# A fused AdaLN, Mamba scan and tree-FFN kernel: softplus of delta straight from PSUM, half of dt in another bank, and three jobs moved in a 32-step schedule

## What is computed

```python
sa, ca, ga, sb, cb, gb = silu(c) @ wmod        # per batch; gates kept at least 0.25 in size
h = layernorm(x) * (1 + ca) + sa
xp, z = split(h @ W_in)                         # 256 channels each
u = silu(causal_depthwise_conv(xp, 4 taps) + conv_b)
dt_r, B, C = split(u @ W_xp, [8, 24])           # rank 8, 16 states for B and for C
delta = softplus(dt_r @ W_dt + dt_bias)
h_t = exp(delta_t * A) * h_(t-1) + delta_t * B_t * u_t      # 256 channels x 16 states
y_t = sum over n of h_t[n] * C_t[n] + u_t * D
x = x + ga * ((y * silu(z)) @ W_out)
h = layernorm(x) * (1 + cb) + sb
gate = sigmoid(h @ (routers Wq))                # 255 nodes of a tree of depth 8
leaf_prob = product of gate or 1 - gate along the path to each of 256 leaves
x = x + gb * (leaf_prob @ leaf_values @ Wout.T + b)
```

## Time and profile before

| | |
|---|---|
| three runs | 538.68 us median (534.51 to 538.88) |
| the profiled execution's own time | 538.69 us |
| its span | 536.9 us |
| mean granted TensorE clock | 0.898 |
| busy: PE, DVE, ACT, POOL | 406.6 (76%), 454.3 (85%), 374.1 (70%), 445.3 us (83%) |
| POOL `hc` L561 | 126 of 2367 ns |
| DVE scan L1286 | 192 of 1270 ns and 64 of 1210 ns |
| DVE `dbu` L1299 | 80 of 1206 ns |
| POOL `dbu` L548 | 48 of 2363 ns |
| ACT exp L649 | 256 of 684 ns |

### The profile page before, as it was taken

How to read it: one execution, slowest core, us unless ns; L and a number is a source line. 1 busy time by engine, 2 the same in 40 slices (tenths; PEclk the granted TensorE clock), 3 DMA queues, 4 the chain that set the end, 5 groups by cost and what they waited for, 6 DMA issues and landing times. The chain is left out here.

```text
span 536.9 us, 6647 instructions
## 1 busy us (share of the span) xinstructions
PE 406.6 (76%) x2104; PEld 278.4 (52%) x2135; DVE 454.3 (85%) x542; ACT 374.1 (70%) x680; POOL 445.3 (83%) x246
## 2 busy tenths in 40 slices
PE   8978834896679757984899747984899758574887
PEld 4436524483548435663567435662557435464554
DVE  6788794998999968998799968997899968998871
ACT  3367774478966888588756898598856886448454
POOL 3468889999899978997799979997889978998800
PEclk8989885899799969998799979999899969785899
DMA  6491062200721073303512063303512063300001
GB/s 169 132 357 75 6 235 89 106 2 21 249 106 62 6 236 117 99 0 125 208 34 89 5 236 117 100 1 131 202 43 81 6 234 118 98 0 2 8 13 39
DMA packets 24867, 53.16 MB, mean 99 GB/s; under 512 B 4601, under 2 KB 13952, under 8 KB 20736
## 3 DMA queue, kind: packets, MB, share of 16 engines
q1 hardware_dynamic: 24832, 52.74, 29.0%
HBM read 50.11 MB, written 2.62 MB: 98 GB/s over the span
## 5 line engine op out<-in xcount | busy, mean ns | idle before, releaser
L561 POOL TENSOR_TENSOR hc<-h,c_rows 128x1024 f32<-128x1024 f32 x126 | 296.6, 2367 | 41.4 <-DVE h L1286 38.0
L1286 DVE TENSOR_TENSOR_SCAN h<-dA,state,dbu 128x512 f32<-128x512 f32 x192 | 234.6, 1270 | 20.1 <-ACT dA L649 19.8
L649 ACT ACTIVATE dA<-delta,a_neg 128x512 f32<-128x512 f32 x256 | 173.1, 684 | 44.5 <-DVE h L1286 43.6
L1065 PE MATMUL yb<-ident,hc 128*128 128x128 f32 x1024 | 155.8, 291 | 22.0 <-POOL hc L561 20.1
L1065 PEld LDWEIGHTS yb<-ident,hc 128*128 128x128 f32 x1024 | 133.3, 152 | 64.7 <-issue 32.4
L548 POOL TENSOR_TENSOR dbu<-du,b_rows 128x1024 f32<-128x1024 f32 x48 | 113.4, 2363 | 4.0 <-DMA b_rows<-bc_dram 4.0
L1299 DVE TENSOR_TENSOR dbu<-du,bb 128x1024 f32<-128x1024 f32 x80 | 96.5, 1206 | 20.5 <-PE bb L1090 10.9
L1286 DVE TENSOR_TENSOR_SCAN h<-dA,dbu 128x512 f32<-128x512 f32 x64 | 74.6, 1210 | 17.8 <-ACT dA L649 17.7
L973 PE MATMUL mf<-f_hT,w_conv 128*128 128x512 f32 x112 | 56.1, 628 | 2.0 <-ACT zu L708 1.4
L996 PE MATMUL mf<-zu,w_xdt 128*128 128x512 f32 x56 | 31.2, 640 | 17.1 <-ACT delta L742 11.5
L824 PE MATMUL mt<-ident,t_xhat 128*128 128x128 f32 x28 | 7.6, 427 | 37.8 <-ACT t_xhat L590 37.8
(11 more groups left out here) (198 smaller groups left out, 544.5 us busy)
## 6 DMA issues: line engine op xcount, KB each, us to landing
c_rows<-bc_dram SPq DMA_DIRECT2D x32, 1024.0 KB, 6.8
b_rows<-bc_dram SPq DMA_DIRECT2D x48, 256.0 KB, 7.3
xs<-in_L_attn_x_dram SPq DMA_DIRECT2D x8, 256.0 KB, 3.8
out_dram<-xs SPq DMA_DIRECT2D x7, 256.0 KB, 5.6
ygT<-in_L_attn_conv_w_dram SPq DMA_DIRECT2D x1, 512.0 KB, 5.1
bc_dram<-xd SPq DMA_DIRECT2D x8, 64.0 KB, 1.6
probT<-in_L_wmod_dram SPq DMA_DIRECT2D x1, 384.0 KB, 4.0
w_in<-in_L_attn_W_in_dram SPq DMA_DIRECT2D x1, 256.0 KB, 4.2
```

The lines of the kernel that those rows point to most:

```text
L561: nc.gpsimd.tensor_tensor(hc[:, pair % RC, :, :], h[:, pair % RH, :, :], c_rows[:, q, n % NQ, :].unsqueeze(1).broadcast_to([P, HALVES, T]) ...
L649: nc.scalar.activation(dA[ke % RD][:, :], delta[:, ge % 2, half, :], ACT.Exp, scale=a_neg[:, half, n:n + 1]).then_inc(s_dA, 1)
L1065: last = nc.tensor.matmul(bank[:, tile], hc[:, pair % RC, half, tile], ident[:, :], start=False, stop=n == N - 1, is_transpose=True, skip_ ...
L1286: v.tensor_tensor_scan(h[:, pair % RH, half, :], dA[k % RD][:, :], dbu[:, pair % RW, half, :], start, ALU.mult, ALU.add).then_inc(s_scan, 1)
```

## The change

Five edits:

1. ACT no longer copies `dt` to SBUF. Softplus with the bias reads the product from PSUM, one instruction per half, at step 17.
2. `dt` half 1 is a job of the t bank (same PE steps 13 and 14), since the f bank now stays occupied by half 0 until step 17. `xd` therefore goes to PE steps 18 and 19 and is read at step 20.
3. The path sums `lp` move to PE steps 19 and 21, `ff` to 23 and 24, the final add to DVE step 24; they now come before the rows' turn: `t_xhat` moves from 19 to 24 (its factor from 15 to 19, POOL's offset from 16 to 20), its `tr` to 27, `node` to 29 and 30.
4. The first norm's statistics of a group are taken one group earlier at step 19 (group 2's before the first scan), and its factor, offset and `f_xhat` at steps 2, 3 and 6.
5. The turns and products of the tail's weights in group 0 move some steps forward.

```diff
-    N_STATS, N_RSTD, N_OFF, N_XHAT = 19, 21, 22, 25
-    F_SILU, F_DT, F_SP, F_DU = 10, (13, 15), 17, (25, 26)
+    N_STATS, N_RSTD, N_OFF, N_XHAT = 19, 2, 3, 6
+    F_SILU, F_SP, F_DU = 10, 17, (25, 26)
-    T_GATE, T_ADD, T_STATS, T_RSTD, T_OFF, T_XHAT = (4, 5), 12, 12, 15, 16, 19
-    U_FIN = 28
+    T_GATE, T_ADD, T_STATS, T_RSTD, T_OFF, T_XHAT = (4, 5), 12, 12, 19, 20, 24
+    U_FIN = 24
     "f": ...
-              ("dt", 0): (1, (11, 12)), ("dt", 1): (1, (13, 14)), ("xd", 0): (1, (15, 16)), ("tr", 0): (2, (28,))},
-        "t": {("yt", 0): (-1, (6,)), ("yt", 1): (-1, (8,)), ("out", 0): (-1, (10,)), ("tr", 0): (-1, (20,)),
-              ("lp", 0): (-2, (22,)), ("lp", 1): (-2, (24,)), ("ff", 0): (-2, (25, 26)), ("node", 0): (-1, (28,)),
-              ("node", 1): (-1, (30,))},
+              ("dt", 0): (1, (11, 12)), ("xd", 0): (1, (18, 19)), ("tr", 0): (2, (28,))},
+        "t": {("yt", 0): (-1, (6,)), ("yt", 1): (-1, (8,)), ("out", 0): (-1, (10,)), ("dt", 1): (1, (13, 14)),
+              ("lp", 0): (-2, (19,)), ("lp", 1): (-2, (21,)), ("ff", 0): (-2, (23, 24)), ("tr", 0): (-1, (27,)),
+              ("node", 0): (-1, (29,)), ("node", 1): (-1, (30,))},
-    W_TURN, W_COPY, W_MUL, W_TAKE, W_SCALE = (4, 9), (7, 11), 13, 16, 20
+    W_TURN, W_COPY, W_MUL, W_TAKE, W_SCALE = (3, 7), (5, 9), 10, 12, 20
...
+        def wait_delta(eng, g, half):
+            if g == 0:
+                eng.wait_ge((s_d0, s_delta)[half], 1)
+            else:
+                wait_read(eng, "ft"[half], "dt", half, g)
...
-                    if front and s in F_DT:
-                        half = F_DT.index(s)
-                        wait_job(act, "f", "dt", half, f)
-                        nc.scalar.activation(delta[:, f % 2, half, :], job("f", "dt", half, f)[1][:, :], ACT.Identity,
-                                             bias=dtb[:, half:half + 1]).then_inc(s_read["f", "act"], 1)
                     if (front or leaf) and s == F_SP:
                         if front:
-
-                            wait_read(act, "f", "dt", 1, f)
-                            both = delta[:, f % 2, :, :]
-                            nc.scalar.activation(both, both, ACT.Softplus).then_inc(s_delta, 1)
+                            for half in range(HALVES):
+                                side = "ft"[half]
+                                wait_job(act, side, "dt", half, f)
+                                nc.scalar.activation(delta[:, f % 2, half, :], job(side, "dt", half, f)[1][:, :],
+                                                     ACT.Softplus, bias=dtb[:, half:half + 1]).then_inc(s_read[side, "act"], 1)
...
-                    if norm and s == N_STATS:
+                    if 2 <= g + 3 < GROUPS and s == N_STATS:
                         dve.wait_ge(s_x, 16 * (GROUPS - 2))
-                        stats(m2, f_bn, f_mv, s_fvar)
+                        if g >= 0:
+                            dve.wait_ge(s_fnm, g + 1)
+                        stats(g + 3, f_bn, f_mv, s_fvar)
```

More of the change, by code:

```diff
@@ L79, in bass_adaln_mamba_tree_ffn_kernel @@
     AHEAD_EXP, AHEAD_FILL, AHEAD_DBU, LAG_SUM = 2, 3, 2, 5
-    N_STATS, N_RSTD, N_OFF, N_XHAT = 19, 21, 22, 25
-    F_SILU, F_DT, F_SP, F_DU = 10, (13, 15), 17, (25, 26)
+    N_STATS, N_RSTD, N_OFF, N_XHAT = 19, 2, 3, 6
+    F_SILU, F_SP, F_DU = 10, 17, (25, 26)
     F_HI, F_R1, F_MID, F_R2, F_LO = 21, 22, 23, 24, 25
-    T_GATE, T_ADD, T_STATS, T_RSTD, T_OFF, T_XHAT = (4, 5), 12, 12, 15, 16, 19
-    U_FIN = 28
+    T_GATE, T_ADD, T_STATS, T_RSTD, T_OFF, T_XHAT = (4, 5), 12, 12, 19, 20, 24
+    U_FIN = 24
     JOBS = {
         "f": {("xp", 0): (1, (0, 1)), ("xp", 1): (1, (3, 4)), ("z", 0): (1, (7,)), ("z", 1): (1, (8,)),
[3 rows of a table removed]
-              ("node", 1): (-1, (30,))},
[3 rows of a table added]
+              ("node", 0): (-1, (29,)), ("node", 1): (-1, (30,))},
     }
     BY_DVE = {"out", "ff"}
+    FIRST_BY_HAND = {("f", "xp"): 1, ("f", "dt"): 1, ("t", "dt"): 1, ("f", "xd"): 1, ("f", "tr"): 2}
     Z_OF_0 = (29, 30)
     TR_OF_1 = STEPS - 1
-    W_TURN, W_COPY, W_MUL, W_TAKE, W_SCALE = (4, 9), (7, 11), 13, 16, 20
+    W_TURN, W_COPY, W_MUL, W_TAKE, W_SCALE = (3, 7), (5, 9), 10, 12, 20
     WARM_START = 9
@@ L112, in bass_adaln_mamba_tree_ffn_kernel @@
             for (name, part), (off, steps) in sorted(JOBS[side].items(), key=lambda job: job[1][1]):
-                first = {"xp": 1, "dt": 1, "xd": 1, "tr": 2}.get(name, 0) if side == "f" else 0
-                if first <= g + off < GROUPS:
+                if FIRST_BY_HAND.get((side, name), 0) <= g + off < GROUPS:
                     job_at[side, name, part, g + off] = len(read_at[side])
@@ L564, in _ @@
                         half = F_DU.index(s)
-                        pool.wait_ge(s_delta, f + 1)
+                        wait_delta(pool, f, half)
                         pool.wait_ge(s_silu, f + 1)
@@ L642, in _ @@
                         if se < HALVES:
-                            act.wait_ge(s_delta, ge + 1)
+                            wait_delta(act, ge, se)
                         if ke >= RD:
@@ L995, in product @@
                         pe.wait_ge(s_silu, g + 1)
+                        if (side, g) == ("t", 1):
+                            pe.wait_ge(s_wtake, 1)
                     last = nc.tensor.matmul(bank[:, :], w_xdt[:, piece, part * P:(part + 1) * P],
```

## The result

The changed kernel takes 516.05 us (median of four runs, 514.96 to 541.32) against 538.36 us for the kernel before, run beside it: a ratio of 0.959, 95% interval 0.954 to 0.965, so 4.1 per cent faster. The forecast was 520.1 us. (The run of 541.32 was disturbed and is left out of the ratio.) The profiled execution took 514.96 us, 23.7 less than the profiled one of before, where the sum said 18.6.

What follows compares the result with a forecast made beforehand. DVE's 53.5 us a cycle plus its stalls was taken as the bound, POOL's 54.0 close under. Gains 14.8 - 0.8 + 2.25 + 1.9 + 0.5 = 18.6 us, from 538.7 to 520.1 us; range 510 to 538.

Steps and rivals of the forecast that it cites:

- Bound: Whole cycle of 60.6 us: DVE's 53.5 us plus its stalls bound it, POOL's 54.0 a floor close under.
- Softplus from PSUM: ACT's block at step 17: 0.6 us pipelined per half, block ends 1.3 us earlier, step 20 stall falls by 1.4.
- Path sums: PE steps 19 to 24: the 2.06 us stall for bb goes; DVE's add waits 1.0 us for ff, bounds nothing and 5.0.
- the hand walk: Group 3 reckoned step by step: ff ready at 260.4, DVE there at 260.0, a wait of 0.5 us at the add.
- First norm: Factor and f_xhat moved to the first half of ACT's cycle: cost nothing; if cover fails, up to 1 us a cycle.
- Sum: Stalls per cycle from 6.6 to 2.9 us (step 20 1.4, ff 1.0, silu 0.5): gain 3.7, cycle 56.9.
- The start's term: Group 2's statistics now ahead of the first dbu: between 0 and 1.6 us lost, 0.8 taken.
- The clock rival: TensorE at 1.2 GHz over lp and ff: DVE waits 5.0 us at the add, no gain, 538 us; chance 0.10.
- Half of it: ACT reads xd and path sums later, the add's wait becomes 3 us, a cycle gains 1.7: 530 us; chance 0.20.
- slower: DVE stands twice around the add, for exp (1.5) and ff (5.0): about 549 us (543 to 553); chance 0.10.
- `xd` late for POOL: xd's later read makes POOL wait for its rows; 9 us of cover against it, counted within the slower case.
- POOL's floor: All stalls but the block's go, POOL hardly waits: 54.5 us a cycle, 508 us; chance 0.05.

Runs made afterwards that it cites:

- the filler products: Ten zero-matrix products on PE at step 18, before xd: changed kernel 521.87 us; dbu before step 20's scan 521.77; that with the add at 26 509.99.
- two edits later: Changed kernel with DVE's dbu ahead of the scan at step 20 and the final add at step 26: 508.19 us, ratio 0.943 to the kernel before.
- the kernel with the `dbu` first: Changed kernel with DVE's dbu ahead of the scan at step 20, add still at step 24: 519.41 us, ratio 0.964 to the kernel before.

## Why the prediction was right, point by point

**Bound.** DVE plus its waits, with POOL close under it: held. DVE's work hardly changed, its waits in four cycles fell by 14.3 us, and POOL's gaps followed.

**Softplus from PSUM.** Taken at 0.6 pipelined, measured 0.58. In group 3 the step-20 stall was to fall to 1.4: it is 1.40. Over the groups it is not so even: 1.40, 1.40, 1.58, 2.58 and 2.58 us in groups 2 to 6. In the last two DVE has no statistics of a coming group left to take at step 19, and stands where in the others it works: I had overlooked that the statistics fill part of the stall, and that one more group is without them after the change. `xd`'s later read cost POOL nothing: no wait for the spread rows is in its list. But the step "its stall falls, so the cycle gains" fails for this edit taken alone (0.1 us a cycle against 1.1 in company): it needs the path sums out of the turn's way.

**Path sums.** The waits at `bb` went, as the hand walk had it, but for one of 0.4 us. The wait at the add was put at 1.0 us, bounds 0 and 5.0, and is 0.23 to 0.72, 0.45 a cycle in the stretch. The walk itself had given 0.5; the doubling I put on it for caution was not needed.

**First norm.** "Cost nothing" holds for the change as a whole, by the run without it. Its silu stall stayed under 1.2 us (0.32 to 1.12), and no wait was added.

**Sum.** Waits 3.0 us a cycle against 2.9. That they agree so well is luck, for the terms do not: step 20 is 1.74 (forecast 1.4), the silu block 0.75 (0.5), `bb` 0.1 (nothing), the add 0.45 (1.0). Three came out too small and one too large by nearly as much. The four cycles gained 16.7 against 14.8: the waits gave 14.3 of it and DVE's work 2.2, where the forecast had only waits. About 1.25 of the work is the set of statistics, for which the stall of group 5 is longer. Outside them the start, forecast at 1.45 with group 1, was measured at 3.4, of which half is no merit of the change (below), and the last group's 0.5 at 1.7, inside its bounds.

Group 0 went as foretold: its long ACT wait (6.28 us in the kernel before) is gone, and DVE stands for POOL in its place, at one scan for POOL's late `dbu` and then for `du` (1.95 in the earlier trace rows):

```profile
85.26 1.22 DVE L1291 TENSOR_TENSOR_SCAN h<-dA,dbu 128x512 f32<-128x512 f32 x1 [8.02 <-POOL dbu L555]
...
92.29 1.22 DVE L1304 TENSOR_TENSOR dbu<-du,bb 128x1024 f32<-128x1024 f32 x1 [2.44 <-POOL du L574]
```

The start's term reckoned with statistics on DVE and not with TensorE's level. The first convolution product in PE's timeline, in the order before, changed, changed with the add at 26:

```profile
32.70 5.40 PE L973 MATMUL mf<-f_hT,w_conv 128*128 128x512 f32 x8 [1.44 <-ACT zu L708]
```

```profile
32.41 3.70 PE L976 MATMUL mf<-f_hT,w_conv 128*128 128x512 f32 x8 [1.22 <-ACT zu L715]
```

```profile
33.93 5.19 PE L976 MATMUL mf<-f_hT,w_conv 128*128 128x512 f32 x8 [1.22 <-ACT zu L715]
```

The granted clock over 28 to 46 us was 0.91, 1.00 and 0.91. The last two kernels issue the same instructions up to there, so this is a matter of the execution. The first scan behind the silu block started at 56.69, 54.72 and 57.72. Between the first and the last, which had the same level here, the change costs 1.0 us at this point (0.8 was forecast for the statistics), and by group 2's block (192.32 and 190.62) it has gained 1.7, close to the 1.45 of the forecast. The profiled execution of the changed kernel stood at 188.92 there. So some 1.7 of its 23.7 us are the level of one execution, and luck.

**Rivals.** The clock rival was real in mechanism and wrong in place: the level falls where I feared, ahead of `xd`, and is back for both path sums (in group 4 during the first), for the reason that I had given against it. Where it was moved onto the second path sum by the filler products, the add's wait was 1.44 us and not 5.0; `ff` ran at 2.4 GHz there (1.06 us). Half of it, slower, and `xd` late for POOL did not come. POOL's floor came, two edits later.

**The loss of the kernel with the `dbu` first.** By its own account it should break even, and its four cycles took 228.8 us against 225.6, with waits of 14.2 against 12.1. Some 3.9 us more at the add stand against 3.9 less at the exp; 2.1 more are at `bb`. PE's timeline of group 3 shows what held a fill up, and DVE's the wait:

```profile
264.43 0.58 PE L1095 MATMUL bb<-b_parts,sel 128*128 128x512 bf16 x1 [3.65 <-DVE dbu L1306]
...
265.66 1.91 PE L1025 MATMUL mt<-t_hT,w_node 128*128 128x512 f32 x2
...
268.26 2.06 PE L1025 MATMUL mt<-t_hT,w_node 128*128 128x512 f32 x2
270.12 0.41 PE L1095 MATMUL bb<-b_parts,sel 128*128 128x512 bf16 x1
```

```profile
270.57 1.22 DVE L1306 TENSOR_TENSOR dbu<-du,bb 128x1024 f32<-128x1024 f32 x1 [0.50 <-PE bb L1095]
```

With the add late, DVE's `dbu` behind it is late too, and PE, done with the turns, stands idle for it: 3.41 to 3.65 us in groups 2 to 5, against 2.64 to 2.84 in the changed kernel. The two node products behind it then take 1.91 and 1.80, 1.91 and 2.06, 1.78 and 1.12, 1.91 and 1.34 us; in the changed kernel they take 1.02 and 1.13, 1.91 and 1.26, 1.02 and 1.12, 1.91 and 1.21 (granted clock here 0.50 over 264 to 268 us). The four cycles are longer than the changed kernel's by 1.4, 1.2, 0.7 and 0.0 us, in the same order. So most of the loss goes with TensorE's level, over the node products and not over `xd`: `xd` is slow there too, but the second path sum starts 8.2 us after the softplus against 8.1. This is read from the traces and tested by no run; the filler products stand ahead of `xd`. That the add at the step of its product is what makes the order tight is shown by moving it (519.4 to 508.2).

## What to carry to other kernels

A stall's price is not its length: the same halved stall was worth 0.1 us a cycle behind one order of PE's queue, and 1.1 us behind another, with a part of the difference in TensorE's level. Follow the chain to the next wait before you book a gain, and remove the wait that all engines share first. A job and its reader in the same step tie two queues together; it may cost little as it stands and still take a later gain, so give it two steps of cover before you tune anything ahead of it. Products that only keep TensorE busy can move its slow stretch to a place where someone waits.

## What the runs showed of the hardware

TensorE's level was low behind quite short waits: granted clock 0.57 in the stretch behind a wait of 2.49 us, 0.62 in the one that holds a wait of 1.97 us. The length of the wait alone does not say whether it falls: in the changed kernel the node products ran at 2.4 GHz behind waits of 2.82 and 2.70 us (groups 2 and 4, 1.02 us for the first two) and at 1.2 GHz behind 2.64 and 2.84 us (groups 3 and 5, 1.91). Executions of the same instructions differ in the level over the first convolution product (3.7 or 5.2 to 5.4 us), and their start by about 3 us (first scan behind the silu block at 54.7 or 54.9 against 57.7); the median hides it and two single profiles do not.
